# A large cross attention with its key path, its query work and half of a running sum moved between engines

## The reference, cut to what matters

```python
sin_k, cos_k = _rope_tables(Lv, D_C)
kv_r = _apply_rope(kv_c, sin_k[None], cos_k[None])
q_r = jnp.einsum('bshq,hqr->bhsr', q_big, W_qr)
k_r = jnp.einsum('bld,hdr->bhlr', kv_r, W_kr)
scores = jnp.einsum('bhsr,bhlr->bhsl', q_r, k_r)
attn = jax.nn.softmax(scores, axis=-1)
ctx_c = jnp.einsum('bhsl,bld->bhsd', attn, kv_r)
ctx_lat = jnp.einsum('bhsd,hkd->bhsk', ctx_c, w_kc_kv)
ctx = ctx_lat.transpose(0, 2, 1, 3).reshape(Bv, Sv, H * K)
return ctx @ Wo.T
```

## Time and profile before

| what | us |
|---|---|
| three timed runs | 3492.21, 3492.59, 3497.96 (median 3492.59) |
| the profiled execution | 3504.15, its span 3501.6 |
| from the first exponents of batch 0 to those of batch 31 | 1835.54 |
| an odd batch (13), an even batch (14), the pair | 70.21, 49.25, 119.46 |

### The profile page before, as it was taken

One profiled execution on the slowest core, in us unless ns is written; L12 is line 12 of the kernel. 1 busy time (PEld: TensorE's weight loads), 2 busy tenths in 40 slices (PEclk: granted clock), 3 DMA queues, 4 the chain that ended last, 5 costly groups with the idle time before them and its releaser, 6 DMA issues. The chain is left out here.

```text
span 3501.6 us, 51568 instructions
## 1 busy us (share of the span) xinstructions
PE 2942.5 (84%) x17592; PEld 1773.8 (51%) x17592; DVE 2084.2 (60%) x3249; ACT 1277.2 (36%) x2482; POOL 900.8 (26%) x784
## 2 busy tenths in 40 slices
PE   6767734579988988898898889888996889999999
PEld 3544412445544544454455445444543457777776
DVE  3445567357686777677776877686775643333332
ACT  3433312123344343434334433444343333333332
POOL 0001000134354444344434544453440000000000
PEclk9888856679999999999999999999999899999999
DMA  1000030000000000000000000000003000000000
GB/s 39 0 17 0 0 117 0 22 19 10 19 9 19 9 19 9 19 9 19 9 11 17 19 9 9 19 9 19 10 0 145 0 0 0 0 0 0 0 0 25
DMA packets 15045, 57.83 MB, mean 17 GB/s; under 512 B 2512, under 2 KB 7248, under 8 KB 13584
## 3 DMA queue, kind: packets, MB, share of 16 engines
q1 hardware_dynamic: 13392, 53.57, 5.5%
q10 hardware_dynamic: 1600, 3.56, 0.3%
HBM read 55.03 MB, written 2.10 MB: 16 GB/s over the span
## 5 line engine op out<-in xcount | busy, mean ns | idle before, releaser
L917 ACT ACTIVATE cx_prob<-cx_st 128x512 f32<-128x512 f32 (+1 forms) x832 | 477.4, 596 | 742.8 <-PE cx_st L774 680.7
L645 POOL TENSOR_TENSOR cx_acc<-cx_acc,cx_prob 128x512 f32<-128x512 f32 (+1 forms) x352 | 493.8, 1403 | 751.5 <-ACT cx_prob L917 747.4
L1023 DVE TENSOR_REDUCE cx_mhalf<-cx_mx 128x1 f32<-128x804 f32 x512 | 491.2, 983 | 86.5 <-PE cx_mx L747 83.7
L785 PE MATMUL cx_av<-cx_prob,cx_kv 128*64 128x512 f32 (+1 forms) x1664 | 462.2, 635 | 0.0
L773 PE MATMUL cx_st<-cx_q,cx_k 128*128 128x512 f32 (+1 forms) x832 | 372.5, 448 | 84.5 <-ACT cx_prob L917 60.5
L1506 PE MATMUL moe_gu<-moe_wgu,moe_xnT 128*128 128x352 f32 x1280 | 399.0, 463 | 0.0
L1044 DVE TENSOR_TENSOR cx_acc<-cx_acc,cx_prob 128x512 f32<-128x512 f32 (+1 forms) x352 | 371.3, 1055 | 21.7 <-ACT cx_prob L917 19.9
L747 PE MATMUL cx_mx<-cx_k,cx_q 128*128 128x402 f32 x1024 | 309.3, 388 | 53.2 <-DVE cx_mhalf L1023 47.3
L1641 DVE SCALAR_TENSOR_TENSOR moe_hid<-moe_silu,moe_coef,moe_gu 128x176 f32<-128x176 f32 x320 | 127.1, 397 | 351.6 <-ACT moe_silu L1569 349.4
L774 PE MATMUL cx_st<-cx_q,cx_k 128*128 128x512 f32 (+1 forms) x832 | 332.8, 400 | 0.0
L747 PEld LDWEIGHTS cx_mx<-cx_k,cx_q 128*128 128x128 f32 x1024 | 173.4, 195 | 264.0 <-DVE cx_mhalf L1023 216.8
(11 more groups left out here) (214 smaller groups left out, 3945.0 us busy)
## 6 DMA issues: line engine op xcount, KB each, us to landing
cx_ctx<-in_cx_ctxT SPq DMA_DIRECT2D x32, 402.0 KB, 4.3
cx_ctxr<-in_cx_ctxrT SPq DMA_DIRECT2D x32, 402.0 KB, 5.5
moe_wgu<-in_moe_wgu SPq DMA_DIRECT2D x5, 1408.0 KB, 15.3
moe_wd<-in_moe_wd SPq DMA_DIRECT2D x4, 896.0 KB, 25.0
x_all<-in_x SPq DMA_DIRECT2D x1, 2048.0 KB, 5.3
cx_wq<-in_cx_wq SPq DMA_DIRECT2D x1, 2048.0 KB, 12.0
cx_woT<-in_cx_woT SPq DMA_DIRECT2D x1, 2048.0 KB, 29.5
out_x<-x_all SPq DMA_DIRECT2D x1, 2048.0 KB, 7.5
```

Of the source, the lines that this page charges most:

```text
L645: pool.tensor_tensor(acc[0][rows, :], sofar, prob[slot(kt)][rows, 0, :], ALU.add)\
L785: last = pe.matmul(av[DCX * p:DCX * p + DCX, :], kv[e][0:nk(kt), kt, :], prob[slot(kt)][0:nk(kt), p, :], start=(kt == 0), stop=(kt == NKT ...
L917: act.activation(prob[slot(kt)][rows, p, :], st[p][rows, :], ACT.Exp).then_inc(s_exp, 1)
L1023: dve.tensor_reduce(mhalf[:, i // 2, i % 2:i % 2 + 1], mx[i % 2][:, :, 0:KQ], AX.XY, ALU.max)\
```

## The change

The keys now come as 13 tiles of 128 keys by 64 numbers, so that POOL's `rotate`, DVE's `sum_keys` and `keep_kl` are one pass of 128x832 instead of chunks on 64 partitions. High and low parts stand side by side in a new tile `khl`. PE turns `khl` with 13 full transposes in four rounds (key tiles 6 to 9) for batch n+2, and ACT keeps each round in a new tile `kp`; the pieces read `kp`. SP copies `kp` to k1 and k2 by two DMAs at the start of the batch before. `values` reads a plain copy of the keys that ACT makes.

The order changes as well. `turn_x` and the queries go from the start of odd batches to the end of key tile 6 and the key tiles 7 to 11 of even batches. The copies of the queries (ACT) and `split` (DVE) come at key tiles 0 to 2 of odd batches. The pieces run in thirds 4 to 21 of even batches and 9 to 30 of odd ones. `normalise` goes from key tile 10 to 5. Last, for key tiles 9 to 12 the running sum of the odd heads is added by POOL (`add_odd`).

```diff
+    SUM_AT = 4
+    NORM_AT = 5
     TURN_AT = 6
+    QUERIES_AT = 7
     ROWS_AT = NKT - 3
-    SUM_AT = (8, 9, 11, 12)
+    HANDED_AT = 9
 
     def pieces(e, kt, third):
 
-        start, end = 3 * (5 if e else 3), 3 * ROWS_AT
+        start, end = (9, 3 * ROWS_AT) if e else (4, 3 * QUERIES_AT)
...
+            def move(n, e):
+
+                sp.wait_ge(s_kp, KROUNDS * (n + 1))
+                if not isinstance(n, int) or n >= 2:
+
+                    sp.wait_ge(s_st, (n - 1) * 2 * NKT)
+                sp.dma_start(k1[e][:, :].bitcast(F32), kp[e][:, 0:SKP].bitcast(F32)).then_inc(s_kd[e], 16)
+                sp.dma_start(k2[e][0:DCX, :].bitcast(F32), kp[e][0:DCX, 0:SKP].bitcast(F32)).then_inc(s_kd[e], 16)
...
+            def rotate(n):
+                pool.wait_ge(s_ctx, 32 * n + 32)
+                pool.tensor_tensor(ctx[:, :, :], ctx[:, :, :], kcos[:, :, :], ALU.mult)
+                pool.tensor_tensor(ctxr[:, :, :], ctxr[:, :, :], ksin[:, :, :], ALU.mult).then_inc(s_rope, 1)
...
+            def add_odd(n, kt):
+
+                rows = slice(0, nk(kt))
+                pool.wait_ge(s_exp, n * 2 * NKT + 2 * kt + 2)
+                pool.wait_ge(s_acc[1], n * NSUM + kt - 1)
+                pool.tensor_tensor(acc[1][rows, :], acc[1][rows, :], prob[slot(kt)][rows, 1, :], ALU.add)\
+                    .then_inc(s_acc[1], 1)
...
+                    if kt >= HANDED_AT:
+                        add_odd(n, kt)
+                    if kt == SUM_AT - 1 and more:
+                        rotate(n + 2)
+                    if kt == NORM_AT and more and e == 0:
...
+            def turn_keys(n, r):
+
+                if r == 0:
+                    pe.wait_ge(s_kl, n + 1)
+                else:
+                    pe.wait_ge(s_kp, KROUNDS * n + r)
+                for kt in range(4 * r, min(4 * r + 4, NKT)):
+                    last = pe.transpose(misc[:, kt % 4 * P:(kt % 4 + 1) * P], khl[:, kt, :, :], ident[:, :])
...
-                    last = pe.matmul(mx[b][:, h, 0:KQ], q, k1[e][:, lo:lo + KQ], start=True, stop=True)
+                    last = pe.matmul(mx[b][:, h, 0:KQ], q, kp[e][:, lo:lo + KQ], start=True, stop=True)
...
-                    if kt == 0 and more and e == 1:
-                        turn_x(t + 1)
...
-                        if more and e == 1 and third < 2 and kt <= CP // 2:
-                            queries(t + 1, 2 * kt + third)
+                            scores(n + 1, t + e, 1 - e, 0, third)
+                        if more and e == 0 and third < 2 and 0 <= kt - QUERIES_AT <= CP // 2:
+                            queries(t + 1, 2 * (kt - QUERIES_AT) + third)
...
+                    if kt == QUERIES_AT - 1 and more and e == 0:
+                        turn_x(t + 1)
...
-                    if kt in (TURN_AT, TURN_AT + 1) and next:
+                    if 0 <= kt - TURN_AT < KROUNDS and more:
...
+            def keep_kh(n):
+                act.wait_ge(s_kr, n + 1)
+                if not is_first(n):
+
+                    act.wait_ge(s_kt, KROUNDS * n)
+                act.copy(khl[:, :, 0, :].bitcast(F32R), kr[:, :, :]).then_inc(s_kh, 1)
...
+                act.copy(kv[e][:, :, :], kr[:, :, :]).then_inc(s_kv, 1)
...
+                act.copy(kp[e][:, 4 * r * P:4 * r * P + w], misc[:, 0:w]).then_inc(s_kp, 1)
...
+                    if kt in (0, 1) and more and e == 1:
+                        keep_queries(t + 1, kt)
+                    if kt == 2 and next:
+                        keep_kv(n + 1, 1 - e)
+                    if kt == SUM_AT and more:
+                        keep_kh(n + 2)
+                    if kt == QUERIES_AT and more and e == 0:
+                        keep_x(t + 1)
+                    if 0 <= kt - TURN_AT - 1 < KROUNDS and more:
+                        keep_turned(n + 2, t + 1, e, kt - TURN_AT - 1)
...
+            def sum_keys(n):
+                dve.wait_ge(s_rope, n + 1)
+                if not is_first(n):
+
+                    dve.wait_ge(s_kv, n)
+                dve.tensor_tensor(kr[:, :, :], ctx[:, :, :], ctxr[:, :, :], ALU.add).then_inc(s_kr, 1)
+
+            def keep_kl(n):
+                dve.wait_ge(s_kh, n + 1)
+                dve.tensor_tensor(khl[:, :, 1, :], kr[:, :, :], khl[:, :, 0, :], ALU.subtract).then_inc(s_kl, 1)
...
-                base = 4 + 6 * t + (4 if e else 0)
+                base = 4 + 6 * t
                 for kt in range(NKT):
                     for third in range(3):
-                        if third == 1 and kt:
+                        if third == 1 and 0 < kt < HANDED_AT:
                             add(n, kt)
-                        if third < 2 and more and e == 1 and kt < CP // 2:
-                            rotate(t + 1, 2 * kt + third)
+                        if third < 2 and more and e == 0 and 0 <= kt - QUERIES_AT < CP // 2:
+                            rotate(t + 1, 2 * (kt - QUERIES_AT) + third)
                         if next:
                             for i in pieces(e, kt, third):
                                 reduce_max(n + 1, i)
                     if kt == 0 and e == 0:
                         odd_queries(t)
-                    if kt == 1 and next:
-                        keep_kl(n + 1, 1 - e)
+                    if kt in (1, 2) and more and e == 1:
+                        split(t + 1, kt - 1)
                     if kt in (HEADS_AT, HEADS_AT + 1) and not is_first(n):
                         invert(n - 1, kt - HEADS_AT)
                         if kt == HEADS_AT + 1:
                             scale_heads(n - 1, 1 - e)
-                    if kt in (3, 4) and more and e == 1:
-                        split(t + 1, kt - 3)
+                    if kt == SUM_AT and more:
+                        sum_keys(n + 2)
+                    if kt == SUM_AT + 1 and more:
+                        keep_kl(n + 2)
                     if kt == OUT_AT + 1 and e == 0 and not is_first(n):
                         update_x(t - 1)
-                    if more and kt in SUM_AT:
-                        sum_keys(n + 2, SUM_AT.index(kt))
-                    if more and e == 0 and kt == ROWS_AT:
-                        normalise(t + 1, base + (2 if next else 0))
+                    if kt == NORM_AT and more and e == 0:
+                        normalise(t + 1, base)
                     if next and kt == ROWS_AT - 1:
-                        negate_max(n + 1, base)
+                        negate_max(n + 1, base + (4 if e else 2 if more else 0))
```

More of the change, by code:

```diff
@@ L494, in context_attention @@
     tab = sb("cx_tab", [P, 2, 3, S])
-    kcos = sb("cx_kcos", [DCX, SKP])
-    ksin = sb("cx_ksin", [DCX, SKP])
-    ctx = sb("cx_ctx", [DCX, SKP])
-    ctxr = sb("cx_ctxr", [DCX, SKP])
-    kr = sb("cx_kr", [DCX, SKP])
+    kcos = sb("cx_kcos", [P, NKT, DCX])
+    ksin = sb("cx_ksin", [P, NKT, DCX])
+    ctx = sb("cx_ctx", [P, NKT, DCX])
+    ctxr = sb("cx_ctxr", [P, NKT, DCX])
+    kr = sb("cx_kr", [P, NKT, DCX])
+    khl = sb("cx_khl", [P, NKT, 2, DCX])
+    kp = [sb(f"cx_kp{i}", [P, SKT], F32R) for i in range(2)]
     k1 = [sb(f"cx_k1{i}", [P, SKP], F32R) for i in range(2)]
@@ L656, in before @@
                 root(0)
-                for n in range(2):
-                    for c in range(NKC):
-                        rotate(n, c)
+                rotate(0)
+                rotate(1)
             def batch(n, t, e, more, next):
@@ L808, in before @@
                 pe.wait_ge(s_one, 1)
-                turn_keys(0, 0)
-                turn_keys(0, 1)
+                for r in range(KROUNDS):
+                    turn_keys(0, r)
                 turn_x(0)
@@ L815, in before @@
                     max_scores(0, 0, 0, i)
-                max_rows(0, 0)
-                max_rows(0, 1)
-                scores(0, 0, 0, 0)
-                scores(0, 0, 0, 1)
+                for r in range(KROUNDS):
+                    turn_keys(1, r)
+                max_rows(0, 0, True)
+                max_rows(0, 1, True)
+                scores(0, 0, 0, 0, 0)
+                scores(0, 0, 0, 0, 1)
             def batch(n, t, e, more, next):
                 for kt in range(NKT):
-                    if kt == 0 and more and e == 1:
-                        turn_x(t + 1)
                     for third in range(3):
@@ L931, in before @@
                 act.wait_ge(s_set, 6)
-                keep_keys(0, 0, k1, s_k1)
-                keep_keys(0, 0, k2, s_k2)
-                keep_kv(0, 0, 0)
-                keep_kv(0, 0, 1)
+                keep_kh(0)
+                keep_kv(0, 0)
+                for r in range(KROUNDS):
+                    keep_turned(0, 0, 0, r)
                 keep_x(0)
@@ L938, in before @@
                     keep_queries(0, g)
+                keep_kh(1)
+                for r in range(KROUNDS):
+                    keep_turned(1, 0, 1, r)
                 keep_rows(0, 0, 0)
@@ L1066, in before @@
                 normalise(0, 0)
-                for c in range(NKC):
-                    sum_keys(0, c)
```

(7 more changed lines are left out.)

131 lines of the change are left out of this document (48 added, 83 removed).

## The result

The changed kernel takes 3629.9 us in the median (3623.6 to 3634.8), the kernel before 3495.3 in the same session: a ratio of 1.038, 95% interval 1.034 to 1.041. It is slower, as forecast, by somewhat less than forecast (3670). The profiled execution has a span of 3632.5 us against 3501.6. Of the 130.9 us between them the cross attention's batches make 128.2: from the first exponents of batch 0 to those of batch 31 it is 1963.8 us now and 1835.6 before (the first exponents of batch 31 start at 2599.54 us; the earlier trace rows ends its stretch at 2599.46).

The account below looks back on a forecast made before the run. PE sets the pace before the change; afterwards DVE bounds even batches up to `turn_x`, then PE alone. Pairs of 130.9 us add 169 us to the batches, +177 with start and end, giving 3670 us, range 3540 to 3790.

Parts of the forecast that it names:

- The pair: Even and odd batch of the cross attention together: 79.1 + 50.1 + 1.7 = 130.9 us, 11.4 more than before.
- DVE's chain up to `turn_x`: Even batch: start at 3.9 us, 33.2 of DVE work, 2.5 of hole, so `turn_x` comes at 39.6 us.
- The query stretch with the last key tile: Even batch from `turn_x` on, bound by PE: 37.2 us, then 3.5 less 1.2 for the last key tile.
- The clock: PE's idle wait before `turn_x` halves its clock: 1.7 us a pair, half of one shortest drop; nothing for the other wait.
- The odd batch: DVE's last reduction ends at 42.4 us, then key tiles 10 to 12 with transposes and rows: 50.1 us.
- The wait in `keep_kh`: Key tile 4: ACT holds key tile 5's exponents until `sum_keys` is done and copied; DVE loses 2.5 us each batch.
- The handing: Sums given to POOL leave DVE mostly where it is idle; at most one of eight leaves its path.
- Batch 0: First batch of the cross attention, without `out` and reciprocals: 75.5 us.
- batch 30: Batch of the cross attention without queries: 46.3 us.
- the end: Batch 31: POOL needs 2.54 us a key tile for two sums against PE's 2.13, about 2 us in all.
- bound by PE: Rival, decided at the wait of `turn_x`: DVE needs less than PE's 24.5 us there, pair 108, 3330 us; chance 0.09.
- DVE runs shorter: Rival: sums near 0.8 us and holes half as long, pair about 124, 3568 us; chance 0.20.
- PE stays slow in the stretches bound by DVE: Rival: half of both stretches at clock 0.50, 8 us a pair, 3790 us; chance 0.14, beyond it 0.04.

Follow-up runs that it names:

- e8: Changed kernel with the queries back in odd batches and no sums handed to POOL: ratio 0.990 to the kernel before, pair 116.73 us.
- e3: Changed kernel with queries, spread of pieces and `normalise` back in their old places, new keys and handing kept: ratio 0.987 to the kernel before, pair 115.87 us.
- e11: Changed kernel with 16 unread matmuls on PE ahead of `turn_x` in even batches: ratio 1.030 to the kernel before, pair 126.24 us.
- e12: e10 with 9 unread matmuls on PE at the end of key tile 4 of odd batches: 3384 us, ratio 0.965 to the kernel before, pair 111.28 us.
- e9: Changed kernel with `sum_keys` and POOL's turning ahead of it one key tile earlier: ratio 1.016 to the kernel before, pair 122.85 us.
- e1: Changed kernel with no sums handed to POOL, DVE adding all odd heads' sums: ratio 1.045 to the kernel before, pair 129.72 us.
- e10: e3 with `sum_keys` and POOL's turning ahead of it one key tile earlier: ratio 0.969 to the kernel before, pair 112.17 us.

## Why the prediction was right, and where its sizes were off

The whole change, taken apart by the means of the pair: 119.70 before, -3.0 for the new way of the keys (e8), -0.9 for the handing (e3 against e8), +12.1 for the place of the queries, with the spread of the pieces and `normalise` that go with it (the changed kernel against e3): 127.98. The signs and the mechanism are as the prediction had them. Its sum gave +169 us for the batches and they measure +128:

- **The pair, 130.9 forecast, 127.98 measured.** The 14 pairs make 41 us of it, and that is nearly all of the miss.
- **DVE's chain up to `turn_x`, 39.6 forecast, 37.7 measured.** The start at 3.9 was right (1663.9 - 1660.0), and so were the work (33.2 with 0.7 of waiting; the 34 instructions in the rows add up to 32.5 without it) and the hole (2.5; 2.67). The step that failed is the sum itself: it added durations, but instructions in a row start before the one ahead has ended (1688.51 + 0.68 = 1689.19, and the next starts at 1689.11). Over 34 instructions that makes 2.2 us: 30.3 busy. This is the largest error, -1.9 of the -2.9 us a pair.
- **The query stretch with the last key tile, 39.5 forecast.** At full clock it is 38.6 (76.46 - 37.81 in e11), 0.9 less.
- **The clock, 1.7 a pair forecast, 1.7 measured** (e11: 2.0 in the even batch, less 0.25 in the odd one). That the numbers agree is luck. It was half of a drop of the shortest kind in one row; the runs have two kinds in turn. The prediction charged nothing for the wait in the odd batch; its clock is 0.93 on average, and no run filled it in the changed order. e12, where filling a wait of 2.8 us at that place in the other order gave 0.9, speaks for a cost. Against it speaks that odd batch 15 of the changed kernel, with 10.2 us at 0.50, is shorter than odd batch 13 with 6.8 us (49.24 and 49.84). It stays open.
- **The odd batch, 50.1 forecast, 49.54 measured.** The last reduction ends at 42.9 (42.4 forecast); behind it 7.0 us, not 7.7.
- **The wait in `keep_kh`.** Forecast: 2.5 us on DVE in each batch. Together it is 5.1 by e9, but unevenly, 3.9 in the odd batch and 1.2 in the even one, where the hole stays (there `turn_x` comes at 36.6 instead of 37.75 us). I had put the hole of the even batch to `out` and `keep_kh` together; e9 shows that without the latter it is as long as before, and filled by `out`.
- **The handing** "at most one of eight": e1 shows one sum of eight ahead of the last reduction, 1.4 us in the odd batch, and 0.3 in the even one by the clock. The sum of POOL's work in the prediction took 26 sums a pair; there are 24, 12 a batch, and nothing hung on it.
- **Batch 0 75.5 (77.64), batch 30 46.3 (44.68), the end +2** (904.2 - 902.1 us behind the first exponents of batch 31: 2.1). The start was to cost 6 us and reads 0.6, but this part varied by 20 us between profiles, so the runs neither confirm nor refute it.

Of the rivals, *bound by PE* failed where the prediction said it would be decided: `turn_x` waited for 5.0 us. *DVE runs shorter* was right in direction, for a reason that it did not name, and too large (124). *PE stays slow in the stretches bound by DVE* happened in small part only: the clock in batch 14 up to `turn_x` is 0.99, and odd batches 13 and 15 run at 0.50 for 6.8 and 10.2 of their 49.8 and 49.2 us, where the rival took half of both stretches. Of the gain that busy times promised, up to 13 us a pair, part exists: 3.8 in e3, 7.5 in e10, 8.4 in e12, where reductions and queries lie in different batches again.

What stays open: whether the hole of 2.6 us that is left in the even batch would go if `out` stood elsewhere, and whether a chain of DVE that met POOL nowhere would keep the new order from losing. Neither was tried.
